# Two softmaxes in a row: scores computed a second time with the row maximum taken off by extra lanes, turns by 64-row halves, and in the wide attention all scores of a pair ahead of its later turns

## What is computed

```
# layer 2, "wide": heads of 64
q, k, v = x @ Wq, x @ Wk, x @ Wv
p = softmax(q k^T * scale + alibi, causal);  x += (p v) Wo + bo
# layer 3, "narrow, twice": heads of 8
s  = q k^T * scale
p1 = softmax(s)
p2 = softmax(p1)
x += p2 v
```

## Time and profile before

| | |
|---|---|
| time, 3 runs | median 2647.92 us (2641.19 to 2651.87) |
| profiled execution | 2653.97 us, its span 2652.2 us |
| mean granted TensorE clock | 0.922 |
| layer 1 attention | about 585 to 990 us of the span |
| layer 2 (wide) attention | about 1135 to 1790 us |
| layer 3 attention | about 1911 to 2562 us, of it 1951.5 to 2557.6 the loop over pairs |

### The profile page before, as it was taken

One profiled execution on the slowest core, in us unless ns is written; L12 is line 12 of the kernel. 1 busy time (PEld: TensorE's weight loads), 2 busy tenths in 40 slices (PEclk: granted clock), 3 DMA queues, 4 the chain that ended last, 5 costly groups with the idle time before them and its releaser, 6 DMA issues. The chain is left out here.

```text
span 2652.2 us, 47713 instructions
## 1 busy us (share of the span) xinstructions
PE 2196.8 (83%) x15155; PEld 1125.9 (42%) x15155; DVE 1958.0 (74%) x5765; ACT 1788.1 (67%) x4541; POOL 988.2 (37%) x1512
## 2 busy tenths in 40 slices
PE   3768785748888888589999999997868888888888
PEld 2446463512222225434444444445334444444453
DVE  4547626759989967768777777776688888888766
ACT  2224223327777774568888878785479999999965
POOL 2643354345445413600000000005645555555437
PEclk8889586759999996799999999999979999999999
DMA  4420514022322310100000000000020111111001
GB/s 140 112 84 13 155 40 135 1 48 59 78 53 55 79 25 1 33 1 1 2 1 1 2 1 2 2 2 1 7 64 1 33 33 33 33 33 33 1 1 32
DMA packets 227640, 94.85 MB, mean 36 GB/s; under 512 B 175746, under 2 KB 215490, under 8 KB 227394
## 3 DMA queue, kind: packets, MB, share of 16 engines
q1 hardware_dynamic: 220864, 83.46, 12.6%
q0 software_dynamic: 3584, 7.58, 1.0%
q10 hardware_dynamic: 2946, 0.77, 0.2%
HBM read 30.66 MB, written 19.17 MB: 19 GB/s over the span
## 5 line engine op out<-in xcount | busy, mean ns | idle before, releaser
L2345 DVE TENSOR_REDUCE s_neg_max<-s_ps_a 128x1 f32<-128x512 f32 x1024 | 662.3, 684 | 141.7 <-PE s_ps_a L2151 129.2
L2613 ACT ACTIVATE s_pT<-s_ps_t 128x512 f32<-128x512 f32 x1024 | 646.1, 659 | 135.8 <-PE s_ps_t L2185 116.4
L2604 ACT ACTIVATE s_first<-s_ps_a,s_neg_max 128x512 f32<-128x512 f32 x512 | 412.0, 805 | 14.0 <-DVE s_neg_max L2345 13.7
L2531 POOL TENSOR_SCALAR s_first<-s_first,s_rec 128x512 f32<-128x512 f32 x384 | 301.6, 801 | 282.6 <-DVE s_rec L2351 282.5
L2197 PE MATMUL s_ps_t<-ident,s_first 128*128 128x128 f32 x2048 | 313.6, 284 | 64.2 <-ACT s_pT L2613 51.2
L2977 DVE CUSTOM_DVE_ANT_0 s_e<-s_ps_a,w_alibi 128x128 f32<-128x128 f32 (+3 forms) x512 | 225.9, 488 | 126.7 <-PE s_ps_a L2813 126.3
L2151 PE MATMUL s_ps_a<-s_lanesT 64*128 64x512 bf16 x1024 | 272.2, 398 | 36.8 <-DMA s_lanesT<-n_lanes 21.2
L2197 PEld LDWEIGHTS s_ps_t<-ident,s_first 128*128 128x128 f32 x2048 | 220.5, 141 | 160.9 <-ACT s_pT L2613 117.4
L2215 PE MATMUL s_ps_o<-s_pT,n_v_pad 128*32 128x512 f32 x2048 | 272.8, 606 | 12.2 <-ACT s_oT L2619 12.2
L3085 ACT ACTIVATE s_e<-s_e,s_neg_max 128x128 f32<-128x128 f32 (+3 forms) x512 | 282.1, 564 | 0.0
L3093 ACT ACTIVATE s_pT<-s_ps_t 128x384 f32<-128x384 f32 (+1 forms) x320 | 156.3, 532 | 115.5 <-PE s_ps_t L2840 88.8
(11 more groups left out here) (428 smaller groups left out, 4138.4 us busy)
## 6 DMA issues: line engine op xcount, KB each, us to landing
s_y_rows<-s_zeros SPq DMA_DIRECT2D x4, 2048.0 KB, 10.0
s_parts<-s_y_rows SPq DMA_DIRECT2D x32, 256.0 KB, 3.8
s_token_rows<-s_rows SPq DMA_DIRECT2D x2, 2176.0 KB, 10.3
s_Wi<-L_ffn_experts_inter SPq DMA_DIRECT2D x2, 1792.0 KB
x<-L_attn_x SPq DMA_DIRECT2D x4, 512.0 KB, 8.1
out<-x SPq DMA_DIRECT2D x8, 256.0 KB, 2.3
s_lanesT<-n_lanes SPq DMA_TRANSPOSE x64, 4.6
s_shiftedT<-n_lanes SPq DMA_TRANSPOSE x64, 2.4
```

The lines of the kernel that those rows point to most:

```text
L2345: dve.tensor_reduce(neg_max[:, column(n):column(n) + 1], sa[n % NA][:], AX.X, ALU.max, negate=True).then_inc(s.max_ready, 1)
L2531: do.free(pool.tensor_scalar(f, f, rec1[:, n:n + 1], 1.0, ALU.mult, ALU.mult))
L2604: act.activation(first[:, g % NF, n % PU, :], sa[n % NA][:], ACT.Exp, bias=neg_max[:, n:n + 1], accum_out=sum1[:, n % (NR * PU):n % (NR * ...
L2613: act.activation(pT[:, n % NP, :], st[n % NK][:], ACT.Exp).then_inc(s.probs_ready, 1)
```

## The change

There are two parts. Layer 1 keeps its order of work.

**Layer 3.** The first exp no longer reads the scores of the matmul that the maximum is taken from, and has no bias. A second matmul computes the scores again with the maximum taken off in three spare lanes (`scores_less_maximum`, into two new banks `less`, tiles `s_ps_m`); for that POOL's `shift` and SP's `turn_shifted` of layer 1 now run in layer 3 too, and there are two lane buffers. The plain scores run 4 pairs ahead (`LAG`) in 2 banks, the second scores and the first exp 2 pairs ahead (`EXP_LAG`). The transposes of a turn go by halves of 64 rows, for both units at once, and both banks `st` are filled by every turn. ACT takes both second exps of a turn, then both first exps.

**Layer 2.** `by_keys(g, 2)` goes into the banks of the even scores, the projections go to the banks of the odd ones, `vo_ps` no longer takes transposes, and the scores of all four blocks stand ahead of `by_keys(g, 1)`.

```diff
-    LAG = 3 if once else 2
+    LAG, EXP_LAG = (3, None) if once else (4, 2)
...
-    NA, NK = (3, 3) if once else (4, 2)
+    NA, NK = (3, 3) if once else (2, 2)
...
+        less = [pb(f"m{i}", [P, 512]) for i in range(0 if once else 2)]
...
                 def bank_free(n):
                     if n >= NA:
-                        pe.wait_ge(s.max_ready if once else s.first_ready, n - NA + 1)
+                        pe.wait_ge(s.max_ready, n - NA + 1)
...
+                def scores_less_maximum(g, t):
+
+                    j, pair = divmod(g, PB)
+                    if t == 0:
+                        pe.wait_ge(shift_turned[g % 2], 16 * (g // 2 + 1))
+                    n = PU * g + 2 * t
+                    if n:
+                        pe.wait_ge(s.first_ready, n)
+                    for a in range(2):
+                        pe.matmul(less[a][:], shiftedT[rows_of(a), g % NS, t * P:(t + 1) * P],
+                                  lanesT[rows_of(a), turned_buffer(j), 1, pair, :], start=True, stop=True).then_inc(s.shifted_psum, 1)
...
+                def by_keys(p, i):
+                    n = PU * p + 2 * i
+                    if n:
+                        pe.wait_ge(s.probs_ready, n)
+                    if i == 0:
+                        pe.wait_ge(s.normal_ready, NORMS_BY_DVE * (p + 1))
+                        pe.wait_ge(s.rest_ready, p + 1)
+                    for a in range(2):
+                        for t in range(TB):
+                            for half in range(2):
+
+                                rows = slice(half * HALF, (half + 1) * HALF)
+                                u = a * TB + t
+                                last = pe.transpose(st[half][:, u * HALF:(u + 1) * HALF],
+                                                    first[rows, p % NF, 2 * t + a, i * P:(i + 1) * P], G.ident[rows, rows])
+                                if u == PU - 1:
+                                    last.then_inc(s.keys_psum, 1)
...
                             if a == 0 and p + LAG < PAIRS:
                                 scores(p + LAG, i)
-                            by_keys(p, i, a)
+                            if a == 0 and p + EXP_LAG < PAIRS:
+                                scores_less_maximum(p + EXP_LAG, i)
+                            if a == 0:
+                                by_keys(p, i)
...
                 def first_exp(n):
-                    act.wait_ge(s.max_ready, n + 1)
+                    act.wait_ge(s.shifted_psum, n + 1)
                     g = n // PU
                     if g >= NF:
                         act.wait_ge(s.keys_psum, PU * (g - NF + 1))
-                    act.activation(first[:, g % NF, n % PU, :], sa[n % NA][:], ACT.Exp, bias=neg_max[:, n:n + 1],
+                    act.activation(first[:, g % NF, n % PU, :], less[n % 2][:], ACT.Exp,
                                    accum_out=sum1[:, n % (NR * PU):n % (NR * PU) + 1]).then_inc(s.first_ready, 1)
...
-        q_ps, k_ps = sa[0]
+        q_ps, k_ps = sa[1]
...
-        HALF_ORDER = (1, 0)
-        turn_bank = lambda m, half: vo_ps if (m, half) == (1, 0) else st[half]
+        turn_bank = lambda m, half: sa[0][half] if m == len(TURNS) - 1 else st[half]
...
                     if m == 1:
...
+                        pe.wait_ge(s.probs_ready, TU * g + 2)
+                    if m == 2 and g + LAG < PAIRS:
+
+                        pe.wait_ge(s.max_ready, PU * (g + LAG) + 6)
...
                     if ahead:
                         scores(g + LAG, 2)
+                        scores(g + LAG, 3)
                     by_keys(g, 1)
-                    if ahead:
-                        scores(g + LAG, 3)
                     by_keys(g, 2)
```

More of the change, by code:

```diff
@@ L2015, in narrow_attention @@
     QUADS = PAIRS // 2
-    NA, NK = (3, 3) if once else (4, 2)
-    NS, NF, NR = 3, 3, 4
+    NA, NK = (3, 3) if once else (2, 2)
+    NS, NF, NR = 3 if once else 2, 3, 4
+    RING = 8
     FIRST = 2
@@ L2100, in turn_shifted @@
                                            ).then_inc(shift_turned[g % 2], 16)
-                rest = slice(FIRST, PB)
                 load(sp)
@@ L2160, in lanes_here @@
                         pe.wait_ge(s.lanes_first, 32 * (g // PB + 1))
-                    if g % PB == FIRST:
-                        pe.wait_ge(s.lanes_turned, 32 * (g // PB + 1))
+                    for pairs, done in zip(PARTS, part_turned):
+                        if g % PB == pairs.start:
+                            pe.wait_ge(done, 32 * (g // PB + 1))
                 def scores(g, t):
@@ L2243, in output @@
                     last.then_inc(s.proj_psum, 1)
-                stir(pe, G, sa[2][:], 8)
+                stir(pe, G, (sa[2] if once else less[0])[:], 8)
                 for j in range(2):
@@ L2252, in _ @@
                         scores(g, t)
+                    if not once and g >= 2:
+                        for t in range(TB):
+                            scores_less_maximum(g - 2, t)
                 pe.wait_ge(s.qkv_added, 2 * TB)
@@ L2555, in _ @@
                     rotate(1, 0)
-                    for g in range(LAG - 1):
-                        shift(g)
-                else:
+                else:
+                    pool.wait_ge(made.lanes_set, 3 * len(G.lanes))
+                    clear_shift(1)
+                for g in range(LAG - 1):
+                    shift(g)
+                if not once:
                     normalise_rest(0)
@@ L2561, in _ @@
                     j, r = divmod(p, PB)
-                    if once and p + LAG - 1 < PAIRS:
+                    if p + LAG - 1 < PAIRS:
                         shift(p + LAG - 1)
@@ L2583, in _ @@
                                 negate_means(j + 2)
-                        if once and r == 6:
+                        if r == 6:
                             clear_shift(j + 2)
@@ L2655, in _ @@
                 else:
-                    for n in range(LAG * PU):
+                    for n in range(EXP_LAG * PU):
                         first_exp(n)
@@ L2662, in _ @@
                         n = PU * p + slot_no
-                        probs(n)
-                        if not once and p + LAG < PAIRS:
-                            first_exp(n + LAG * PU)
+                        if once:
+                            probs(n)
+                        elif slot_no % 2 == 0:
+                            probs(n)
+                            probs(n + 1)
+                        if not once and p + EXP_LAG < PAIRS:
+                            first_exp(n + EXP_LAG * PU)
                         if once and slot_no == 2 and p % 2 and p >= 3:
```

147 lines of the change are left out of this document (80 added, 67 removed).

## The result

The changed kernel takes 2933.39 us (median of 4 runs, 2933.04 to 2933.74), the kernel before 2644.56 (4 runs, 2625.0 to 2651.87): a ratio of 1.109, 95% interval 1.105 to 1.113. The prediction was 2900, within 2845 to 3000. The profiled execution took 2933.04 us for a span of 2930.8, at a mean granted clock of 0.872 where it was 0.922.

The account below looks back on a forecast made before the run. ACT was taken to bound layer 3's loop and PE the wide loop. The terms 228 + 2 + 27 - 12 = +245 us on the profiled 2653.97 gave 2899, the median 2893, put at 2900; 8 in 10 within 2845 to 3000.

Parts of the forecast that it names:

- five steps: Layer 3 loop: first exps of one turn, then second scores, transposes, second exps, first exps of the next, none overlapping.
- ACT's waits once a turn: Sign in layer 3's loop: ACT waits about 1.3 us once a turn before the second exps, on the transposes.
- PE's wait for the first exps: Sign in layer 3's loop: PE waits on the first exps before the second scores, once a turn.
- The cycle's size: Layer 3 loop: 3.30 us a turn against 2.39 before, over 248 turns +228 us.
- Bias, read, handover and exps: Layer 3 cycle: bias 0.09, accumulator read 0.09, handovers 0.27 and 0.04, two second exps 0.96, last first exp 0.48 us.
- the second scores: Layer 3 cycle: two 64-row matmuls side by side, 0.32 us until the next PE work starts.
- Rival 2: Layer 3's chain, but PE's clock falls in its gaps: 3080 us if always low, 2990 if half; chance 0.12.
- the 1.00 that the forecast said the profile must show: Sign in layer 3's loop: a granted clock of 1.00.
- Ahead of the loop: Layer 3 before its loop: 44 us instead of 17, and 0.5 for clearing the second lane buffer; +27 us.
- The wide loop: Layer 2's loop: PE loses up to 0.3 us less in each pair; -12 us, bounds -20 and +15.
- The open choice: Layer 3's first exps: the trace didn't split 0.09 us between bias and accumulator; all was taken as bias.
- Rival 3: Layer 3: second scores not late, ACT stays the bound, dropping the bias gives -46 us; whole 2617 us; chance 0.04.

Follow-up runs that it names:

- e1: The changed kernel with the transposes ahead of the second scores in PE's turn of layer 3: 2666.74 us, ratio 1.008 to the kernel before.
- e2: The kernel before with layer 3's scores in a ring of two banks instead of four, and `stir`'s bank to match: 2983.26 us, ratio 1.129.
- e5: The changed kernel plus four bf16 matmuls, results overwritten, ahead of the plain scores in every second turn of layer 3: 2917.41 us, ratio 1.095.
- e3: The changed kernel with the wide loop as in the kernel before, so the change in layer 3 alone: 2943.62 us, ratio 1.113.
- e4: The changed kernel with layer 3 as in the kernel before, so the change in the wide layer alone: 2639.93 us, ratio 0.997.
- e8: The kernel before with layer 3's first exps given a constant scale instead of the bias operand, accumulator kept: 2638.26 us, ratio 0.989.
- e9: e7 with PE's turn reordered to transposes, plain scores, second scores, and four products every turn instead of eight every second turn: ratio 1.029.
- e6: e1 with each score matmul waiting for its own bank alone instead of both for both banks: ratio 0.998.
- e7: e6 with turns of plain scores and of second scores alternating ahead of layer 3's loop: ratio 0.998.
- e10: e7 with the plain scores behind the transposes in the second and fourth turn of a pair: ratio 1.001.

## Why the prediction was right

**The mechanism held.** A cycle through five steps, none overlapping another. e1 removes the one edge that closes it (transposes behind second scores) and the time is back; e2 adds the edge alone and the time is gone. The profile shows what it named: ACT's waits once a turn, two first exps 0.58 apart, no DMA or POOL at the end of PE's waits. PE's wait for the first exps came in 174 of the 248 turns and not in each: behind products at the low clock PE comes to the second scores without waiting.

**The cycle's size.** Predicted 3.30 us, measured 3.21 at the high clock. Bias, read, handover and exps came out within 0.02. What was too long is the second scores, 0.32 until the next work, measured 0.22 to 0.23: I took the 0.32 from a place where the next work had been full transposes, and half transposes follow closer. The e2 rows bear that out: with full transposes the distance is 0.32 again (2301.72 to 2302.04). The mean turn of e5 is 3.25 with ACT's copies in it, so over the loop the chain was put at 15 us too much: the forecast of 605.5 + 230 against e5's 821.0.

**The clock.** Rival 2, to which I gave 0.12, was partly true: the granted clock was 0.82 over the loop, not the 1.00 that the forecast said the profile must show. The sum had put this term at nothing. It costs 43 us (864.4 against 821.0), for a rival that I had priced at +90 for half the time low. I had argued that the same work fills more of a turn at the low clock and so brings the clock back. The mean of 0.82 says that it does so only in part: turns at either level stand next to each other. In most turns the products' longer time costs nothing, since it lies in ACT's. What counts is, in the 75 of 239 turns whose second scores run at the low clock, 0.18 more from these to the transposes (0.40 for 0.22) and 0.28 more from the transposes to ACT's start (0.98 for 0.70 in the mean; the turn shown above, with 0.90, is one of the shorter). Such a turn takes 3.73 us where the others of ordinary length take 3.24: 75 x 0.49 = 37 us. Six turns of 4.45 us, one for each sequence projected in the loop, add 7: there a projection of 1.65 us and products of 1.8 us stand ahead of the second scores, and PE is the late one. I had priced the two distances at +0.22 and at +0.51, the latter from full transposes instead of halves, and had not priced the six turns.

The two errors have opposite signs: the chain was put 15 us too long, the clock 43 too short. So the loop was forecast at +230 and came to +259, and these 29 are nearly all of the 33 us that the prediction missed. That the chain's error took a third off the clock's is luck. The Trainium skill, page "TensorE: Matmul & The Clock Gate", section "A second HAM failure mode: psum-queue depth-cycling", describes such a swing between the levels caused by short idle times between matmul groups. The rows agree with it: 0.82 in after, where PE waits 1 to 1.9 us at a time, and 0.98 in e5, where part of that idle time is filled.

**Ahead of the loop.** Forecast 44 us, measured 43.4. The turns came as added up: a turn of plain scores 1.98 to 1.99 us (2.0 forecast), a turn of second scores 1.96 (1.95):

```profile
1934.24 0.61 PE L2171 MATMUL s_ps_a<-s_lanesT 64*128 64x512 bf16 x2 [1.37 <-DVE s_neg_max L2401]
1936.23 0.61 PE L2171 MATMUL s_ps_a<-s_lanesT 64*128 64x512 bf16 x2 [1.38 <-DVE s_neg_max L2401]
1936.63 0.64 PE L2203 MATMUL s_ps_m<-s_lanesT,s_shiftedT 64*128 64x512 bf16 x2
1938.62 0.61 PE L2203 MATMUL s_ps_m<-s_lanesT,s_shiftedT 64*128 64x512 bf16 x2 [1.35 <-ACT s_first L2665]
1940.58 0.61 PE L2203 MATMUL s_ps_m<-s_lanesT,s_shiftedT 64*128 64x512 bf16 x2 [1.36 <-ACT s_first L2665]
```

**The wide loop.** Forecast -12, measured -10.2 here and by e3 against after, -8.5 in e4, -7 in the mean of all profiled executions. The size held; that the gain is the waiting that the sum named is not shown (see e3 and e4).

**The bias.** The open choice, all 0.09 us to the bias and none to the accumulator, was right (after's own rows and e8). Rival 3, the gain of 46 us, would not have been had in full even without the chain: e8 gets 25 of it, and e1, with all second scores in place, 6.

**Not in the sum.** Stages that the change does not touch add +3.6 us (-11.7 + 1.7 + 13.6). That it is so little is chance: the first of them alone differs by 28 us between the profiled executions.

## What to carry to other kernels

Where an engine's queue holds two kinds of work, write down for each piece which result it needs, and look whether a piece that could go now stands behind one that needs the newest result of the engine it feeds. If so, both engines take turns, and the cycle can be added up from start-to-start distances of rows of the old trace, to 3% here; the cure is the order of the queue, not less work. A lag of two pairs on paper is worth nothing when the wait is on the last instruction issued and the ring of banks holds one turn.

Once a chain opens gaps on TensorE, ask what they do to its clock, and don't count matmuls that run side by side as if they took turns: half of them may take the whole time.

## What the runs showed of the hardware that was not expected

- Eight f32 products of 128x32 by 512 columns, four heads' worth, take 1.06 us; four of them, two heads' worth, take 1.05 us (e9).
- With four extra bf16 matmuls of 512 columns (1.03 us) in every second turn the granted clock in the loop is 0.98 instead of 0.82 and the loop 43 us shorter, one profiled execution of each (e5).
- The same code at the end of the program takes 93 to 96 us in the profiled executions of before, e2, e5, e6 and e9 and 107 to 109 us in those of after, e1, e3, e4, e7, e8 and e10. In the long ones some 24 us pass at the low clock while TensorE is busy throughout. First the kernel before, then the kernel after, at the same place behind their last transposes:

```profile
2569.00:2581.00 12.00, 12.00 (x94) 10.46 (x93) 9.17 (x55) 3.78 (x7) 5.77 (x6) 1.00 0.00 0
```

```profile
2834.00:2846.00 12.00, 12.00 (x53) 10.65 (x54) 7.65 (x52) 1.79 (x3) 6.09 (x7) 0.50 0.00 0
2846.00:2858.00 12.00, 12.00 (x50) 10.20 (x49) 4.10 (x15) 1.99 (x4) 0.00 (x0) 0.50 0.00 1
```

  That e4, whose layer 3 is that of the kernel before, is among the long ones says that it is not layer 3's code that decides. What does was not tried. It is 13 us, half a per cent, and may be a part of the spread of the runs of one kernel.
